# Attention layer of a two-layer kernel: values' high and low parts in one product, the last low part by ScalarE and GpSimd

## The reference

```python
h = _group_norm(x, gn_w, gn_b)
hf = h.reshape(B, C, N)                                  # B 8, C 512, N 1024
qkv = jnp.einsum('oc,bcn->bon', qkv_w, hf) + qkv_b[None, :, None]
qkv = qkv.reshape(B, 3, NUM_HEADS, HEAD_DIM, N)          # 8 heads of 64
q, k, v = (qkv[:, 0], qkv[:, 1], qkv[:, 2])
attn = jnp.einsum('bhdi,bhdj->bhij', q, k) * HEAD_DIM ** (-0.5)
attn = jax.nn.softmax(attn, axis=-1)
out = jnp.einsum('bhij,bhdj->bhdi', attn, v)
out = out.reshape(B, C, N)
out = jnp.einsum('oc,bcn->bon', proj_w, out) + proj_b[None, :, None]
return x + out.reshape(B, C, H, W)
```

## Time and profile before

| | us |
|---|---|
| median of 3 runs | 2717.58 |
| lowest, highest | 2716.95, 2725.69 |
| profiled execution, span of the core | 2718.4 |
| busy in it: TensorE, VectorE, ScalarE, GpSimd | 2619.7, 2055.1, 1578.5, 221.9 |

### The profile page before, as it was taken

The page is one execution under the profiler, slowest core; times in us unless marked ns, Lnnn a source line. Parts: engine busy times, 40 slices in busy tenths (PEclk is TensorE's granted clock), DMA queues, the critical chain, the costliest instruction groups (busy, mean ns, idle before and its releaser), DMA issues.

```text
span 2718.4 us, 33180 instructions
## 1 busy us (share of the span) xinstructions
PE 2619.7 (96%) x11856; PEld 2181.7 (80%) x11856; DVE 2055.1 (76%) x3294; ACT 1578.5 (58%) x1930; POOL 221.9 (8%) x134
## 2 busy tenths in 40 slices
PE   6999999999999999999999999999999987899998
PEld 5788888888888888888888888888888876688887
DVE  6788768876887688768876887688767867878864
ACT  4667646764676467646764676567646663334311
POOL 1000000000000000000000000000000012111010
PEclk9999999999999999999999999999999999899999
DMA  4512232223222322232223222321322335466444
GB/s 156 177 50 80 67 103 61 79 71 100 64 78 67 101 67 76 63 107 67 65 72 109 66 59 79 109 67 48 90 83 58 112 127 203 171 215 246 165 164 170
DMA packets 154849, 279.48 MB, mean 103 GB/s; under 512 B 51776, under 2 KB 52032, under 8 KB 154176
## 3 DMA queue, kind: packets, MB, share of 16 engines
q1 hardware_dynamic: 152128, 268.98, 31.4%
q0 software_dynamic: 2560, 8.39, 1.0%
HBM read 180.04 MB, written 63.18 MB: 89 GB/s over the span
## 4 chain that ended last, share of the span: by engine, by line
PE 83%; DVE 9%; issue 3%; DMA 2%; ACT 1%; SPq 0%; POOL 0%; POOLq 0%; DVEq 0%; ACTq 0%
PE tiles L372 9%; PE tiles L373 8%; PE tiles L374 8%; PE tiles L474 8%; PE tiles L451 8%; PE tiles L428 8%; PE tiles L468 8%; PE tiles L467 8%; PE tiles L447 7%; PE tiles L1321 5%; PE tiles L1371 2%; DVE row_max L679 2%; DVE p_low L695 2%; DVE h_low L787 1%; PE tiles L383 1%
## 5 line engine op out<-in xcount | busy, mean ns | idle before, releaser
L679 DVE TENSOR_REDUCE row_max<-tiles 128x1 f32<-128x512 f32 x1014 | 694.5, 685 | 443.4 <-PE tiles L428 440.6
L544 ACT ACTIVATE p_high<-tiles 128x1024 fp32r<-128x1024 f32 x512 | 525.5, 1026 | 595.8 <-PE tiles L451 595.1
L695 DVE TENSOR_TENSOR p_low<-tiles,p_high 128x1024 fp32r<-128x1024 f32 x512 | 623.0, 1217 | 7.0 <-ACT tiles L546 6.2
L546 ACT ACTIVATE tiles<-tiles 128x1024 f32<-128x1024 f32 x512 | 523.0, 1021 | 0.0
L467 PE MATMUL tiles<-p_high,v_high 128*128 128x512 f32 x1024 | 406.5, 397 | 2.2 <-ACT num_den L562 1.5
L428 PE MATMUL tiles<-k_high_low,q_high_high 128*128 128x512 f32 x1014 | 404.8, 399 | 0.2 <-DVE row_max L679 0.2
L468 PE MATMUL tiles<-p_high,v_low 128*128 128x512 f32 x1024 | 402.0, 393 | 0.0
L428 PEld LDWEIGHTS tiles<-k_high_low,q_high_high 128*128 128x128 f32 x1014 | 312.5, 308 | 48.6 <-DVE row_max L679 5.7
L474 PE MATMUL tiles<-p_low,v_high 128*128 128x512 f32 x1024 | 325.8, 400 | 14.9 <-DVE p_low L695 14.6
L451 PE MATMUL tiles<-q_low_max,k_high_one 65*128 65x512 f32 x1024 | 325.8, 399 | 1.9 <-DMA q_low_max<-row_max_top 1.8
L372 PE MATMUL tiles<-h_high,w_high 128*128 128x512 f32 x768 | 304.6, 397 | 17.3 <-DVE row_max L679 8.3
(11 more groups left out here) (167 smaller groups left out, 3138.1 us busy)
## 6 DMA issues: line engine op xcount, KB each, us to landing
x_tiles<-in_x SPq DMA_DIRECT2D x64, 512.0 KB, 5.4
w_high<-w_split SPq DMA_DIRECT2D x126, 256.0 KB, 2.8
w_low<-w_split SPq DMA_DIRECT2D x126, 256.0 KB, 3.0
k_high_one<-k_high_low SPq DMA_DIRECT2D x128, 128.0 KB, 2.3
q_high_high<-q_high_high SPq DMA_DIRECT2D x128, 128.0 KB, 2.3
o_normed<-rec_rows SPq DMA_DIRECT2D x64, 256.0 KB, 3.7
x<-x_tiles SPq DMA_DIRECT2D x32, 512.0 KB, 4.0
x_full<-x SPq DMA_DIRECT2D x32, 512.0 KB, 8.3
```

The costliest lines, as they stand in the source:

```text
L544: nc.scalar.activation(ph[:, r, :], ring[:, r, :], ACT.Exp, scale=ATT_SCALE).then_inc(s_ph, 1)
L546: nc.scalar.activation(ring[:, r, :], ring[:, r, :], ACT.Exp, scale=ATT_SCALE).then_inc(s_p32, 1)
L679: nc.vector.reduce_max(mcol[:, h % 2, n, i:i + 1], max_bank(h, i, n)[:, :], AX_X).then_inc(s_mx, 1)
L695: tt(pl[:, r, :], ring[:, r, :], ph[:, r, :].bitcast(F32), ALU.subtract).then_inc(s_pl, 1)
```

## The change

Per head the weights are now 128 columns of another kind (`v_parts`): 64 columns of values' high parts, 63 of their low parts, and one column of ones. One product with `p_high` gives what two gave, and the denominator is one row instead of 64. `p_low` is multiplied by the same weights. Two things are then left over.

- Rows 0 to 62 of the second block are the low part's share of the numerator. VectorE adds them after the copy out of `pv` (`add_low`, signalled by `s_num`, for which `weigh_high` and `normalise` now wait instead of `s_nd`).
- The 64th column's low part has no place among the weights. It is kept as a column in `v_low_last`. For each tile ScalarE multiplies the first 512 of `p_high` by it (`last_term`, after the step's other copies) and GpSimd the second 512 (`last_term_odd`); GpSimd adds both, and the tiles before, in `add_terms` (128 x 1024, in steps 1, 2, 3 of each half head), and after the fourth tile two more products on TensorE (in `weigh_low`) add the sum to the numerator's 64th row through the weights `pick_last`, which are zero but for one column of ones.

Around that: GpSimd's `normalise` moves between the additions of step 6 and step 7; the output projections move one step later each; `o_high` goes from step 7 of a pair's even head to step 0 of the odd head, `o_low` from step 0 to step 1; the maximum over two halves is a reduction with one input instead of an operation with two; some steps of SyncE's stores move by one. `bank_events` counts 3 instead of 5 products for the order in which PSUM banks are given out.

```diff
--- before.py
+++ after.py
@@ -72,9 +72,10 @@
         kind = g % PAIRS
         if kind == 0 and g > 0:
             o = [("o", b0 - 1, t, i) for t in range(CT) for i in range(2)]
-            for s in range(7):
-                put(b, 1 + s, o[s])
-            put(a + 2, 0, o[7])
+            for s in range(6):
+                put(b, 2 + s, o[s])
+            for s in range(2):
+                put(a + 2, s, o[6 + s])
         if n == ALL_PAIRS:
             continue
...
-    v2 = sb("v_low", [P, 2, NT, 3, HD], F32R)
+    vw = sb("v_parts", [P, 2, NT, 4, HD], F32R)
+    pick, v_last = sb("pick_last", [P, 3 * HD], F32R), sb("v_low_last", [P, 2, NT, 2])
+    sb("spare", [P, 800])
...
-    sb("spare", [P, 2, N])
+    term = sb("last_terms", [P, 2, N])
...
             last.then_inc(s_sc, 1)
 
-        def weights_of(v, t, n):
+        def weights_of(t, n):
             h, j = t // STEPS, 2 * (t % 4) + n
-            return v[:, (h // 2) % 2, j, h % 2:h % 2 + 2, :].rearrange("p a d -> p (a d)")
+            return vw[:, (h // 2) % 2, j, 2 * (h % 2):2 * (h % 2) + 2, :].rearrange("p a d -> p (a d)")
 
         def weigh_high(t):
             if t % 4 == 0 and t > 0:
-                pe.wait_ge(s_nd, t // 4)
+                pe.wait_ge(s_num, t // 4)
             if t % (2 * STEPS) == 0:
                 pe.wait_ge(s_vl, vt(("vt", t // (2 * STEPS), 1)))
             pe.wait_ge(s_ph, t + 1)
             for n in range(2):
-                p = ph[:, t % 2, n * HALF:(n + 1) * HALF]
-                mm(pv[:, :], weights_of(v1, t, n), p, start=(t % 4 == 0 and n == 0), stop=False)
-                last = mm(pv[:, :], weights_of(v2, t, n), p, start=False, stop=False)
+                last = mm(pv[:, :], weights_of(t, n), ph[:, t % 2, n * HALF:(n + 1) * HALF],
+                          start=(t % 4 == 0 and n == 0), stop=False)
             last.then_inc(s_phu, 1)
 
         def weigh_low(t):
             pe.wait_ge(s_pl, t + 1)
+            odd = (t // STEPS) % 2
             for n in range(2):
-                last = mm(pv[:, :], weights_of(v1, t, n), pl[:, t % 2, n * HALF:(n + 1) * HALF],
-                          start=False, stop=(t % 4 == 3 and n == 1))
+                last = mm(pv[:, :], weights_of(t, n), pl[:, t % 2, n * HALF:(n + 1) * HALF],
+                          start=False, stop=False)
+            if t % 4 == 3:
+                pe.wait_ge(s_sum, 3 * (t // 4 + 1))
+                for n in range(2):
+                    last = mm(pv[:, :], pick[:, 0:P] if odd else pick[:, HD:HD + P], last_sum[:, n * HALF:(n + 1) * HALF],
+                              start=False, stop=(n == 1))
             last.then_inc(s_plu, 1)
 
...
@@ -541,9 +555,21 @@
             act.wait_ge(s_sc, t + 1)
             if t > 1:
                 act.wait_ge(s_phu, t - 1)
+                act.wait_ge(s_term_odd, t - 1)
             nc.scalar.activation(ph[:, r, :], ring[:, r, :], ACT.Exp, scale=ATT_SCALE).then_inc(s_ph, 1)
 
             nc.scalar.activation(ring[:, r, :], ring[:, r, :], ACT.Exp, scale=ATT_SCALE).then_inc(s_p32, 1)
+
+        def last_term(t):
+
+            h, j = t // STEPS, 2 * (t % 4)
+            act.wait_ge(s_ph, t + 1)
+            if t % (2 * STEPS) == 0:
+                act.wait_ge(s_vl, vt(("vt", h // 2, 1)))
+            if sums_before(t) > 0:
+                act.wait_ge(s_sum, sums_before(t))
+            nc.scalar.activation(term[:, int(t % 4 > 0), 0:HALF], ph[:, t % 2, 0:HALF].bitcast(F32), ACT.Copy,
+                                 scale=v_last[:, (h // 2) % 2, j, h % 2:h % 2 + 1]).then_inc(s_term, 1)
 
         def product_high(n):
...
@@ -632,7 +659,7 @@
                 normed_high(b, s - 5)
             if h % HEADS == 6 and b < BATCH and s == 0:
                 normed_high(b, CT - 1)
-            if h % 2 == 0 and h > 0 and s == 7:
+            if h % 2 == 1 and h > 1 and s == 0:
                 o_high(h // 2 - 1)
             if t + EARLY < len(FRESH):
...
                 dve.wait_ge(s_mrow[i], 16 * (h - 1))
-            tt(mtop[:, h % 2, blocks], mcol[:, h % 2, 0, blocks], mcol[:, h % 2, 1, blocks], ALU.max
-               ).then_inc(s_mtop, 1)
+            nc.vector.reduce_max(mtop[:, h % 2, blocks], mcol[:, h % 2, blocks, :], AX_X).then_inc(s_mtop, 1)
 
         def p_low(t):
             r = t % 2
@@ -713,9 +739,22 @@
         def v_low(u):
             n, i = u[1], u[2]
             dve.wait_ge(s_vh, vt(u))
+            if n == 0:
+                dve.wait_ge(s_pset, 5)
             js = slice(4 * i, 4 * i + 4)
-            tt(v2[:, n % 2, js, 0:3:2, :], fill_of(u)[:, :].rearrange("p (j a d) -> p j a d", j=4, a=2),
-               v1[:, n % 2, js, 0:3:2, :].bitcast(F32), ALU.subtract).then_inc(s_vl, 1)
+            turned = fill_of(u)[:, :].rearrange("p (j a d) -> p j a d", j=4, a=2)
+            high = vw[:, n % 2, js, 0:4:3, :].bitcast(F32)
+            tt(vw[:, n % 2, js, 1:3, 0:HD - 1], turned[:, :, :, 0:HD - 1], high[:, :, :, 0:HD - 1], ALU.subtract)
+            tt(v_last[:, n % 2, js, :], turned[:, :, :, HD - 1], high[:, :, :, HD - 1], ALU.subtract).then_inc(s_vl, 1)
+
+        def add_low(n):
+
+            h, i = n // 2, n % 2
+            a = h % 2
+            cols = slice(i * HALF, (i + 1) * HALF)
+            rows, others = slice(a * HD, a * HD + HD - 1), slice((1 - a) * HD, (1 - a) * HD + HD - 1)
+            dve.wait_ge(s_nd, n + 1)
+            tt(nd[rows, a, cols], pv[others, :], nd[rows, a, cols], ALU.add).then_inc(s_num, 1)
 
         def product_low(n):
...
@@ -808,6 +847,8 @@
                     if done[1] % 4 == 3:
                         top_of_halves(done[0], done[1] // 4)
                 p_low(t - 1)
+                if t % 4 == 1 and t > 1:
+                    add_low(t // 4 - 1)
             if block:
                 reduce_max(*block, 0)
             if t > 0:
@@ -822,7 +863,7 @@
                     normed_low(b, s - 6)
                 if h % HEADS == 6 and s < 2:
                     normed_low(b, s + 2)
-            if h % 2 == 1 and h > 1 and s == 0:
+            if h % 2 == 1 and h > 1 and s == 1:
                 o_low(h // 2 - 1)
             if h > 0 and s == 3:
...
             nc.gpsimd.tensor_tensor(gs[:, 5, :], gs[:, 4, :], gs[:, 0, :], ALU.pow).then_inc(s_rstd, 1)
 
-        nc.gpsimd.memset(v1[:, :, :, 1, :].bitcast(F32), 1.0).then_inc(s_pset, 1)
+        def last_term_odd(t):
+
+            h, j = t // STEPS, 2 * (t % 4) + 1
+            pool.wait_ge(s_ph, t + 1)
+            if t % (2 * STEPS) == 0:
+                pool.wait_ge(s_vl, vt(("vt", h // 2, 1)))
+            if sums_before(t) > 0:
+                pool.wait_ge(s_sum, sums_before(t))
+            nc.gpsimd.tensor_scalar(term[:, int(t % 4 > 0), HALF:N], ph[:, t % 2, HALF:N].bitcast(F32),
+                                    v_last[:, (h // 2) % 2, j, h % 2:h % 2 + 1], None, ALU.mult).then_inc(s_term_odd, 1)
+
+        def add_terms(t):
+
+            pool.wait_ge(s_term, t + 1)
+            pool.wait_ge(s_term_odd, t + 1)
+            if t % 4 == 3 and t > 3:
+                pool.wait_ge(s_plu, t - 3)
+            nc.gpsimd.tensor_tensor(last_sum[:, :] if t % 4 == 3 else term[:, 0, :], term[:, 0, :], term[:, 1, :],
+                                    ALU.add).then_inc(s_sum, 1)
+
+        nc.gpsimd.memset(pick[:, :].bitcast(F32), 0.0).then_inc(s_pset, 1)
         pool.wait_ge(s_pset, 1)
-        nc.gpsimd.memset(v2[:, :, :, 1, :].bitcast(F32), 0.0).then_inc(s_pset, 1)
-        pool.wait_ge(s_pset, 2)
+        for i in range(2):
+            nc.gpsimd.memset(vw[:, i, :, 1:3, HD - 1].bitcast(F32), 1.0).then_inc(s_pset, 1)
+        nc.gpsimd.memset(pick[:, P - 1:P].bitcast(F32), 1.0).then_inc(s_pset, 1)
+        pool.wait_ge(s_pset, 4)
         nc.gpsimd.memset(k2[HD:HD + 1, :, :].bitcast(F32), -1.0).then_inc(s_pset, 1)
-        pool.wait_ge(s_pset, 3)
+        pool.wait_ge(s_pset, 5)
         pool.wait_ge(s_dset, 1)
         rstd(0)
-        for h in range(1, ALL_HEADS):
-            b = h // HEADS + 1
-            if h % HEADS == 5 and b < BATCH:
-                rstd(b)
-            normalise(h - 1)
+        for h in range(ALL_HEADS):
+            for s in range(STEPS):
+                t = h * STEPS + s
+                last_term_odd(t)
+                if t % 4 > 0:
+                    add_terms(t)
+                if h > 0 and s == 6:
+                    pool.wait_ge(s_sum, sums_before(t + 1))
+                    normalise(h - 1)
+                    pool.wait_ge(s_on, h)
+                if h % HEADS == 4 and s == 7 and h // HEADS + 1 < BATCH:
+                    rstd(h // HEADS + 1)
+        pool.wait_ge(s_sum, 3 * TILES // 4)
         normalise(ALL_HEADS - 1)
         then(pool)
```

31 lines of the change are left out of this document (18 added, 13 removed).

## The result

The changed kernel takes 2987.22 us (median of 4 runs, 2986.38 to 2990.44) against 2719.53 for the kernel before: ratio 1.0986, 95% interval 1.0971 to 1.1002. It is 268 us slower. The forecast was 2775 with a range of 2690 to 2840: the sign was right, the size was not. The profiled execution has a span of 2984.3 us.

What follows compares the result with a forecast made beforehand. TensorE's instruction count bounds the kernel now; after the change, a loop through GpSimd every four tiles. Batches 1 to 6 +34, last +4 and +13, first +7, end +2: +60 on 2717.6, stated as 2775 us, range 2690 to 2840.

Steps and rivals of the forecast that it cites:

- the loop: Every four tiles, TensorE's next scores wait behind GpSimd's sum; a half takes the longer of this and TensorE's count; chance 0.62.
- the signs I named: In the layer: sum's products wait 1 to 4 us, GpSimd 65 to 80% busy, TensorE about 88%, second halves longer.
- the multiplication: GpSimd's new 128x512 operation per tile: 0.85 us, between 0.48 and 1.20 (half an addition).
- 16.0 + u: Second half of a head: the loop's length in us; u is the projection ScalarE copies there, 0 to 1.3.
- Hand-overs: Between GpSimd's operations in the loop: 0.08 us each, taken from two memsets.
- First halves: First half of a head, without the normalisation: 13.5 us plus ScalarE's projection copy, mostly hidden behind TensorE's 15.2.
- The last pair's four loops: Last batch's last pair, without projections: from at least 45 us to loops of 13.5 + 16.0 a head, 59: +13.
- The first batch: The batch with no output projections to gain from: +7 us.
- kind 2's odd second half: Second half of kind 2's odd head: 19.0 us, ScalarE's busy time in that head being 34.0, with waits 35.6.
- ScalarE's side of the loop: Three ScalarE copies wait in the loop for the addition before, the next tile's exponentials queued behind; no size given.
- the loop hides: Rival: GpSimd's additions well under 2.4 us, so TensorE's count rules: 2590 us, half of it 2680; chance 0.18.
- Port: VectorE's two-input SBUF operations meet GpSimd 13 times a batch: 2.6 us; as rival about 2835 us and beyond, chance 0.10.

Runs made afterwards that it cites:

- e1: Changed kernel without the 64th low part's path (no ScalarE copies, GpSimd terms or additions, or products of the last sum): 2634.7 us, 0.9686.
- e6: e1 plus ScalarE's copy in each tile, waiting for no sum and its result unused: 2658.32 us, 0.9781.
- e5: e1 plus GpSimd's multiplications and additions, on zeros, nobody waiting but TensorE once at the layer's end: 2674.06 us, 0.9843.
- e11: Changed kernel plus ten idle TensorE products ahead of the wait of each head's second half: 2947.12 us, 1.0833.
- e3: Changed kernel with GpSimd's multiplication written as two tensors, the second a column read again and again: 2879.22 us, 1.0597.
- e4: Changed kernel with GpSimd's normalisation after the last addition; o_high, o_low, output projections and two stores one step later: 2851.67 us, 1.0487.
- e10: Changed kernel with e3, e4, alternating term buffers, sum's products behind next scores and row maximum, group scale and kind 1 projections later: 2772.99 us, 1.0205.
- e2: Changed kernel without TensorE's wait and two products of the last sum per half head; ScalarE's and GpSimd's work stays: 2914.76 us, 1.0723.
- e12: e1 without VectorE's add_low too, so weigh_high waits for ScalarE's copy alone: 2563.34 us, 0.9422.

## Why the prediction was wrong in size

**The account.** After minus before is 268 us: -85 for the rest of the change (e1), +352 for the 64th low part. Of the 352, 58 are the products of the sum, 24 ScalarE's copies (e6), 39 GpSimd's load beside VectorE (e5), and 231, the remainder, I put down to the waits of the loop, which hold what the clock costs (e11, 40 or more). That the loop costs most of this is shown by e3, e4 and e10, which shorten it and take 108, 136 and 214 us off; the 231 itself is a remainder and no run measures it. e10 comes within 17 us of the sum of the parts, with some of the loop's waits still in it.

**The mechanism** was named rightly: products of the last sum wait for GpSimd's addition, ScalarE's copies wait for the same, TensorE's share in the layer falls to 88% (2127 of 2412), GpSimd is busy 79%, an addition takes 2.4 us. Two of the signs I named were off: TensorE waits up to 6.2 us, not 4, though mostly at tile 1 of a head as said (188 of 215 us), and second halves are longer than first ones only in kind 3 and in the odd heads of kinds 1 and 2. The saving on TensorE was also right in products: -1024 and +256.

**The term that failed is the multiplication.** I bounded it by "not over half an addition, 1.20", which assumes that one tensor input costs no more per element than two. It took 1.56, 0.71 over my value. No row of before showed such an operation, and a bound from another kind of operation was no bound. The sum gave a second half 16.0 + u; with 2 x 0.71 more it is 17.4 + u. It isn't the whole miss: e3, with a multiplication of 1.04, is still at 2879 us, above my range. The page "GPSIMD Engine Reference" of the Trainium skill, section 3.1, gives 769 ns as measured for 512 elements, in the best case of a loop; this trace shows about twice that for the multiplication.

**Hand-overs** on GpSimd were put at 0.08, from two memsets. Quiet stretch of the changed kernel, timeline of GpSimd:

```profile
1467.30 1.56 POOL L936 TENSOR_SCALAR last_terms<-p_high,v_low_last 128x512 f32<-128x512 f32 x1 [0.17 <-POOL last_terms L945]
```

Between additions and multiplications 0.14 to 0.18 us pass (0.08 to 0.10 on either side of the normalisation), which adds some 0.3 to the loop: 17.7 + u.

**First halves** I took to hide mostly, 13.5 + u behind TensorE's 15.2. With both corrections the loop is 13.5 + 1.4 + 0.3 = 15.2 + u, and it no longer hides. From tile 1 to tile 5 and so on (even head first and second half, odd head first and second), by the starts of each tile's first score product in the traces, medians over batches 1 to 6:

| pair kind | predicted us | before | after |
|---|---|---|---|
| 0 | 18.4, 16.6, 20.6, 20.7 | 19.8, 17.0, 22.0, 22.0 | 20.8, 18.2, 21.5, 20.7 |
| 1 | 18.0, 17.2, 17.2, 16.6 | 16.6, 16.7, 17.1, 14.3 | 18.8, 18.8, 17.7, 18.3 |
| 2 | 14.8, 16.0, 16.6, 19.0 | 15.9, 15.9, 17.1, 14.1 | 17.9, 17.9, 17.5, 21.7 |
| 3 | 15.6, 17.3, 15.7, 16.6 | 15.9, 16.6, 17.1, 15.7 | 17.4, 19.4, 18.6, 18.7 |

A batch takes 303.8 us, not 276.9. Fifteen of the sixteen halves are over the forecast, by 0.5 to 3.1 us; only the odd head's second half in kind 0, with the most TensorE work of its own, came as said. The last pair's four loops, from the products of one last sum at 2406.12 to those at 2480.98, took 74.9 us where I said 59; the corrected loop gives 66. The first batch took 42 us more than before, where I had said 7.

**How much each is of the 212 us by which I missed.** By e3's share, 81% of a cut in the loop, 2 x 0.71 x 128 would be some 148 us, and 0.3 x 128 some 30. This is worked out, not measured, and it overlaps with the clock. The table says more. Of the 27 us a batch, 11.0 lie in the six second halves where the loop was forecast to rule, and there the forecast with 1.7 us added comes within 0.4 us of each: this part is the multiplication and the hand-overs. 13.3 lie in the eight first halves. There 15.2 + u in place of 13.5 + u explains at most 3.4, as in the other five something else was the longer in the forecast. e11 takes 6.5 off the first halves: that is the lower clock, of which the prediction has no word. The last 2.7 lie in kind 2's odd second half, which was forecast from ScalarE's busy time. About 6 us a batch are thus left, in that half and in the first halves. Of these, 1.4 are TensorE's own count (below); the cause of the others stays open. (The sum itself, 2717.6 + 60, is 2778; I had written 2775.)

**ScalarE's side of the loop** stood in the prediction with the exponentials queued behind the copies, but had no price. e2 shows that it closes the loop by itself, through the copy out of `pv` and `add_low`. `add_low` I priced at 0.7 us of VectorE's time and almost nothing on the path; it was 71 us of path (e12). Where the loop rules this is hidden. It isn't in the first halves of the odd heads of kinds 0 and 1: they take 21.5 and 17.7 us, which is e1's 21.0 and 17.2 with 0.46 for the sum's two products, and I had 20.6 and 17.2. So TensorE's own count was too low as well: "the loop hides", put at 2590, would have been about 2693 at the least (e1 with the 58 us of products), a gain of 1%.

**ScalarE's copy** shows 0.72 us (0.62 net of the overlap of 0.1; 0.60 forecast). **Port.** The rule of the Trainium skill's page "SBUF — State Buffer", section "Who interferes with whom", agrees with this trace: beside GpSimd `h_low` takes up to 2.13 us instead of 1.21, and above, at 1488.88, the normalisation takes 3.23 instead of 2.40 beside `h_low`. But only 41 of the 512 multiplications were lengthened, by some 33 us together. e5 puts GpSimd's load without the loop at 39 us, some 5 a batch where the forecast had 2.6, so that rival was at most a small part of the miss. Its rows of up to 3.6 us for `h_low` and `o_low` didn't occur. **GpSimd's spans.** The Trainium skill's page "Perfetto Trace Analysis", section "GPSIMD Engine Instruction", calls them unreliable; here they agree with the starts that follow them, and with e3's gain.

## What to carry to other kernels

Before work goes to an idle engine, write out the loop that it closes, with a row for each operation in it; where no row shows an operation, no other kind of operation bounds it: here 512 elements took 1.56 us in the multiplication and 1024 took 2.40 in the addition. Time it by itself, or let the range hold twice its price. Take the loop through every queue that waits for its end: here TensorE and ScalarE each closed it, so that freeing one gave 14 us (72 less the products' 58) or 20. And run the change first without its left over part: e1 showed a gain of 85 us, against 138 us for the rest in the best form tried (e10).

## What the runs showed of the hardware that I had not expected

- On GpSimd a product of 128x512 with a column per partition took 1.56 us as tensor with scalar, and 1.04 as tensor with a column read again and again (e3), so the form with one tensor input is the slower.
- An addition of 128x1024 took 1.93 us where both inputs were the same place, with zeros in it (e5), 2.4 where they were two; which of the two made the difference was not tested.
- Between an addition and a multiplication on GpSimd, the second waiting for the first, 0.14 to 0.18 us pass; about the normalisation, which waits likewise, 0.08 to 0.10.
- After waits of 4 to 6 us TensorE's products went at 0.43 us instead of 0.23, at the 1.2 GHz level; ten unneeded products ahead of each head's longest wait took most of that away and gave 40 us back (e11).
